# A two-layer transformer kernel on one core: the third batch's down products move out of the first attention unit into the order of the FFN chunks, with the first layer's front reordered

## The reference, cut to what matters

```
xn = layernorm(x)
attn: qkv = xn @ qkv_w + qkv_b   (16 heads of 64), causal softmax(q k / 8) v, @ out_w + out_b
ffn:  gate = xn @ w_gate / 127;  up = xn @ w_up / 127;  (silu(gate) * up) @ w_down / 127   (384 hidden)
x = x + attn + ffn
```

## Time and profile before

| | |
|---|---|
| median of 3 runs | 1658.24 us (1657.25 to 1658.27) |
| the profiled execution | 1658.69 us, span 1657.0 us |
| PE busy | 1636.4 us, 99% of the span |
| DVE, ACT, POOL busy | 80%, 61%, 54% |
| mean granted clock of PE | 0.999 |

### The profile page before, as it was taken

The page is one execution under the profiler, slowest core; times in us unless marked ns, Lnnn a source line. Parts: engine busy times, 40 slices in busy tenths (PEclk is TensorE's granted clock), DMA queues, the critical chain, the costliest instruction groups (busy, mean ns, idle before and its releaser), DMA issues.

```text
span 1657.0 us, 29205 instructions
## 1 busy us (share of the span) xinstructions
PE 1636.4 (99%) x9922; PEld 1043.9 (63%) x9922; DVE 1328.9 (80%) x2763; ACT 1006.7 (61%) x2025; POOL 888.1 (54%) x686
## 2 busy tenths in 40 slices
PE   8999999999999999999999999999999999999998
PEld 6756556655665566566656665665666767676767
DVE  6677777777777778777777777776999999999997
ACT  4456666656665666566656666666676657566562
POOL 3233333334333333433333433334999999999995
PEclk9999999999999999999999999999999999999999
DMA  8000000000000000000000000000000000000000
GB/s 182 26 1 1 2 1 1 1 2 1 1 1 1 1 2 1 1 1 1 1 1 1 1 2 1 1 27 1 1 1 7 7 1 8 5 4 7 1 8 13
DMA packets 30036, 13.55 MB, mean 8 GB/s; under 512 B 17066, under 2 KB 29380, under 8 KB 29892
## 3 DMA queue, kind: packets, MB, share of 16 engines
q1 hardware_dynamic: 29892, 11.70, 3.0%
HBM read 9.60 MB, written 2.10 MB: 7 GB/s over the span
## 4 chain that ended last, share of the span: by engine, by line
PE 92%; DVE 4%; ACT 1%; issue 1%; POOL 1%; DMA 0%; SPq 0%; DVEq 0%; ACTq 0%; POOLq 0%
PE pair L994 17%; PE flip L1011 16%; PE accum L1032 11%; PE pair L2739 8%; PE misc L959 7%; PE flip L2762 4%; PE misc L1078 4%; PE flip L2751 4%; PE misc L972 3%; PE accum L1056 3%; PE flip L2799 3%; PE accum L2751 2%; PE accum L2762 2%; PE accum L1060 2%; PE flip L2785 1%; PE flip L936 1%
## 5 line engine op out<-in xcount | busy, mean ns | idle before, releaser
L388 POOL TENSOR_SCALAR probs<-probs,recip 128x256 f32<-128x256 f32 (+5 forms) x448 | 331.3, 754 | 687.5 <-DVE recip L642 687.4
L463 ACT ACTIVATE probs<-pair,neg_max 128x768 f32<-128x768 f32 (+5 forms) x448 | 332.0, 749 | 208.4 <-DVE neg_max L624 208.4
L624 DVE TENSOR_REDUCE neg_max<-pair 128x1 f32<-128x768 f32 (+7 forms) x512 | 372.8, 754 | 31.4 <-PE pair L994 9.5
L1011 PEld LDWEIGHTS flip<-ident,probs 128*128 128x128 f32 x2048 | 228.0, 141 | 142.3 <-issue 64.7
L994 PE MATMUL pair<-qk_sb 64*128 64x512 f32 (+3 forms) x1536 | 291.6, 505 | 1.4 <-ACT probs L463 0.7
L1011 PE MATMUL flip<-ident,probs 128*128 128x128 f32 x2048 | 280.0, 277 | 1.8 <-ACT slots L425 1.8
L425 ACT ACTIVATE slots<-flip 128x512 f32<-128x512 f32 x320 | 183.6, 595 | 155.5 <-PE flip L1011 155.5
L615 DVE TENSOR_TENSOR pair<-pair,mask 128x128 f32<-128x128 f32 x512 | 137.2, 292 | 80.4 <-PE pair L994 80.3
L1032 PE MATMUL accum<-slots,v_sb 128*64 128x512 f32 (+3 forms) x1024 | 192.7, 519 | 0.0
L2739 PE MATMUL pair<-slow_sb,h_T 128*128 128x512 f32 x384 | 180.0, 594 | 1.2 <-ACT probs_last L463 1.0
L1571 POOL TENSOR_TENSOR prod<-xnT,qs 128x1024 f32<-128x1024 f32 (+3 forms) x32 | 180.2, 5638 | 0.9 <-DVE qs L2280 0.9
(11 more groups left out here) (230 smaller groups left out, 2539.7 us busy)
## 6 DMA issues: line engine op xcount, KB each, us to landing
out<-x SPq DMA_DIRECT2D x8, 256.0 KB, 2.3
x<-in_L_attn_x SPq DMA_DIRECT2D x3, 512.0 KB, 5.8
slow_sb<-in_L_attn_w_slow SPq DMA_DIRECT2D x3, 512.0 KB, 7.5
w_qk<-in_L_attn_qkv_w SPq DMA_DIRECT2D x2, 512.0 KB, 7.2
xn<-in_L_ffn_W SPq DMA_DIRECT2D x1, 1024.0 KB
x<-in_L_attn_x SPq DMA_DIRECT2D x2, 256.0 KB, 3.3
w_v<-in_L_attn_qkv_w SPq DMA_DIRECT2D x1, 512.0 KB, 7.5
bv_bc<-in_L_attn_qkv_b SPq DMA_DIRECT2D x1, 512.0 KB, 7.5
```

The costliest lines, as they stand in the source:

```text
L388: pool.tensor_scalar(part, part, recip[:, u % 2, row, h:h + 1], 0.0, ALU.mult, ALU.add).then_inc(scaled, 1)
L463: act.activation(dst, pair[h][:, lo:hi], ACT.Exp, bias=neg_max[:, u % 2, row, h:h + 1], accum_out=row_sum[:, u % 2, row, h:h + 1]).then_in ...
L624: dve.tensor_reduce(out=neg_max[:, u % 2, row, h:h + 1], in_=pair[h][:, lo:hi], axis=AX.X, op=ALU.max, negate=True).then_inc(max_ready, 1)
L1011: last = pe.transpose(flips[bank][:, P * k:P * (k + 1)], src[:, P * k:P * (k + 1)], ident[:])
```

## The change

It does seven things, all in the first layer:

1. PE: `branch(2)` leaves unit 0; its halves stand in the front, the first after the gate product of chunk (3, 1), the second after the last product. DVE's `add_branch(2)` leaves unit 0 likewise, in halves.
2. PE: `hidden` can issue the gate and the up product separately, and `flip_xn` a half at a time; projections, down products and transposes stand between the products.
3. PE: `project(0, 0, 1)` and `project(0, 1, 0)` come much earlier, with the wait for the q and k weights; the values products come earlier as well.
4. DVE: `norm` goes by halves, each with its own signal, so that transposes of a half wait for that half alone; `keep_lo` goes by halves; `statistics(2)` precedes `multiply(0, 0)`, and `statistics(3)` `multiply(1, 1)`.
5. ACT: `keep_hi` goes by halves; the order of silus and copies follows that of PE. A Silu of one column is put first.
6. POOL: `deviation(1)` and `deviation(2)` come before the wait for `out_b`, `deviation(3)` behind `add_bias(2)`; `add_bias(b)` waits for both halves of its own norm.
7. Waits of `flip_xn` are by half too: for batch 1 on the half's copy of batch 0, for later ones on the half's addition of two batches before.

No instruction is left out; one is added (the small Silu). The diff, without the bodies of `norm`, `keep_lo`, `keep_hi` and `hidden`, which get the half or the product as an argument and are otherwise as they were:

```diff
@@ POOL
             def add_bias(b):
-                pool.wait_ge(xn_ready, min(b + 2, B))
+                pool.wait_ge(xn_ready, 2 * b + 1)
...
+            deviation(1)
+            deviation(2)
             pool.wait_ge(small_loaded, 16)
-            for b in range(1, B):
-                deviation(b)
-                add_bias(b - 1)
-            add_bias(B - 1)
+            add_bias(0)
+            add_bias(1)
+            add_bias(2)
+            deviation(3)
+            add_bias(3)
@@ ACT
+            act.wait_ge(ident_made, 1)
+            act.activation(act_gate[:, 0:1], ident[:, 0:1], ACT.Silu)
             act.wait_ge(ints_loaded, 48)
...
             keep_hi(0)
             silu(0, 0)
             silu(0, 1)
-            keep_hi(1)
+            keep_hi(1, (0,))
+            keep_hi(1, (1,))
             silu(0, 2)
             keep_xnT(1)
             silu(1, 0)
             silu(1, 1)
-            keep_hi(2)
+            keep_hi(2, (0,))
+            keep_hi(2, (1,))
             silu(1, 2)
             keep_xnT(2)
+            silu(2, 0)
+            keep_hi(3, (0,))
+            silu(2, 1)
+            keep_hi(3, (1,))
+            silu(2, 2)
+            silu(3, 0)
+            keep_xnT(3)
             act.wait_ge(bq_scaled, 1)
-            silu(2, 0)
-            silu(2, 1)
-            keep_hi(3)
-            silu(2, 2)
-            keep_xnT(3)
-            silu(3, 0)
             keep_part(0, 1, 1)
@@ DVE
                 maximum(u, 7, 0)
-                if u == 0:
-                    add_branch(B - 2)
...
             statistics(1)
+            statistics(2)
             multiply(0, 0)
-            norm(1)
+            norm(1, 0)
+            norm(1, 1)
             multiply(0, 1)
-            keep_lo(1)
-            statistics(2)
+            keep_lo(1, 0)
+            keep_lo(1, 1)
+            dve.wait_ge(bq_scaled, 1)
+            keep_part(0, 0, 1)
             multiply(0, 2)
-            norm(2)
+            keep_part(0, 1, 0)
+            norm(2, 0)
+            norm(2, 1)
+            add_branch(0, (0,))
             multiply(1, 0)
-            add_branch(0, (0,))
+            statistics(3)
+            add_branch(0, (1,))
             multiply(1, 1)
-            add_branch(0, (1,))
-            keep_lo(2)
+            keep_lo(2, 0)
+            keep_lo(2, 1)
+            multiply(1, 2)
+            norm(3, 0)
+            norm(3, 1)
             dve.wait_ge(v_loaded, 32)
-            dve.wait_ge(bq_scaled, 1)
-            statistics(3)
-            multiply(1, 2)
-            norm(3)
+            keep_values(0, 0)
             multiply(2, 0)
-            keep_part(0, 0, 1)
             add_branch(1, (0,))
+            add_branch(1, (1,))
+            keep_lo(3, 0)
             multiply(2, 1)
-            add_branch(1, (1,))
-            keep_part(0, 1, 0)
-            keep_lo(3)
+            keep_lo(3, 1)
+            keep_values(0, 1)
             multiply(2, 2)
-            keep_values(0, 0)
             multiply(3, 0)
-            keep_values(0, 1)
+            add_branch(2, (0,))
             multiply(3, 1)
             multiply(3, 2)
+            add_branch(2, (1,))
@@ PE
+                    else:
+                        pe.wait_ge(xn_ready, 2 * b + f)
+                    if b == 1:
+                        pe.wait_ge((xnT_dve, xnT_act)[f], 1)
+                    elif b:
+                        pe.wait_ge(ffn_added, 2 * (b - 2) + f + 1)
...
                 score(u, 0, 0)
-                if u == 0:
-                    branch(B - 2)
...
-            flip_xn(0)
-            hidden(0, 0)
-            hidden(0, 1)
-            flip_xn(1)
-            hidden(0, 2)
-            hidden(1, 0)
+            flip_xn(0, (0,))
+            flip_xn(0, (1,))
+            hidden(0, 0, (0,))
+            hidden(0, 0, (1,))
+            hidden(0, 1, (0,))
+            hidden(0, 1, (1,))
+            flip_xn(1, (0,))
+            hidden(0, 2, (0,))
+            flip_xn(1, (1,))
+            pe.wait_ge(qk_loaded, 32)
+            project(0, 0, 1)
+            hidden(0, 2, (1,))
+            hidden(1, 0, (0,))
+            project(0, 1, 0)
             pe.wait_ge(xnT_act, 2)
             branch(0, (0,))
-            hidden(1, 1)
+            hidden(1, 0, (1,))
+            hidden(1, 1, (0,))
             branch(0, (1,))
-            flip_xn(2)
-            hidden(1, 2)
-            pe.wait_ge(qk_loaded, 32)
+            hidden(1, 1, (1,))
+            flip_xn(2, (0,))
+            flip_xn(2, (1,))
+            hidden(1, 2, (0,))
+            hidden(1, 2, (1,))
             pe.wait_ge(v_loaded, 32)
-            project(0, 0, 1)
-            hidden(2, 0)
+            project_values(0, 0)
+            hidden(2, 0, (0,))
+            hidden(2, 0, (1,))
             pe.wait_ge(xnT_act, 3)
             branch(1, (0,))
-            hidden(2, 1)
             branch(1, (1,))
-            project(0, 1, 0)
-            flip_xn(3)
-            hidden(2, 2)
-            project_values(0, 0)
+            flip_xn(3, (0,))
+            hidden(2, 1, (0,))
+            flip_xn(3, (1,))
+            hidden(2, 1, (1,))
+            hidden(2, 2, (0,))
+            project_values(0, 1)
+            hidden(2, 2, (1,))
+            hidden(3, 0, (0,))
+            project(0, 1, 1)
+            hidden(3, 0, (1,))
+            hidden(3, 1, (0,))
             pe.wait_ge(xnT_act, 4)
-            hidden(3, 0)
-            project_values(0, 1)
-            project(0, 1, 1)
-            hidden(3, 1)
+            branch(2, (0,))
+            hidden(3, 1, (1,))
             project(0, 0, 0)
-            hidden(3, 2)
+            hidden(3, 2, (0,))
+            hidden(3, 2, (1,))
+            branch(2, (1,))
```

More of the change, by code:

```diff
@@ L522, in keep_xnT, with keep_hi @@
                 act.activation(xnT[:, b, 512:1024], flips[1][:], ACT.Copy).then_inc(xnT_act, 1)
-            def keep_hi(b):
+            def keep_hi(b, halves=(0, 1)):
                 if b == 0:
@@ L531, in keep_hi @@
                     act.wait_ge(up_ready, NHID * (b - 1))
-                for f in range(2):
+                for f in halves:
                     act.wait_ge(xn_flipped, 2 * b + f + 1)
@@ L786, in first_norm, with norm @@
                 last.then_inc((xn_first, xn_ready)[f], 1)
-            def norm(b):
+            def norm(b, f):
                 dve.wait_ge(rstd_ready, b + 1)
@@ L791, in norm @@
                     dve.wait_ge(xn_flipped, 2 * (b - 1))
-                for r in range(ROWS):
+                for r in range(GB * f, GB * (f + 1)):
                     last = dve.tensor_scalar(xn[:, b % 2, r, :], x1[:, b, r, :], mv[:, b, r, 0:1], rstd[:, b, r:r + 1],
@@ L799, in keep_xnT, with keep_lo @@
                 dve.tensor_copy(xnT[:, b, 0:512], flips[0][:]).then_inc(xnT_dve, 1)
[L801 to L805, removed]
+            def keep_lo(b, f):
+                part = slice(512 * f, 512 * (f + 1))
+                dve.wait_ge(hi_kept, 2 * b + f)
+                dve.tensor_tensor(lo_T[b % 2][:, part], flips[f][:], hi_T[b % 2][:, part].bitcast(F32), ALU.subtract).then_inc(lo_dve, 1)
             def multiply(b, j):
@@ L879, in _, with flip_xn @@
             pe.transpose(pair[1][:, 512:512 + COLUMNS], stage[:], ident[0:COLUMNS, 0:COLUMNS]).then_inc(setup_flipped, 1)
[L881 to L886, removed]
+            def flip_xn(b, halves=(0, 1)):
+                for f in halves:
                     if b == 0:
                         pe.wait_ge((xn_first, xn_ready)[f], 1)
+                    else:
[4 more added lines that the diff above has]
+                        pe.wait_ge(ffn_added, 2 * (b - 2) + f + 1)
                     for r in range(GB):
@@ L891, in flip_xn, with hidden @@
                     last.then_inc(xn_flipped, 1)
-            def hidden(b, j):
+            def hidden(b, j, products=(0, 1)):
                 n = b * NHID + j
-                for h, w_T in enumerate((gate_T, up_T)):
+                for h in products:
+                    w_T = (gate_T, up_T)[h]
                     if h == 0 and n:
```

## The result

The changed kernel takes 1654.61 us (median of 12 runs, 1653.23 to 1656.12) where the one before takes 1657.79 (12 runs, 1657.21 to 1660.29) in the same sitting. The ratio is 0.9979, with a 95% interval from 0.9971 to 0.9987: faster by 0.2%, and by 3.2 us from median to median. The forecast was 1652.5, 2.1 us too low, with a range up to 1655.5.

The account below looks back on a forecast made before the run. TensorE (PE), busy 99% of the span, was taken as the bound. A gain of 7.2 less 1.55 for the clock, 5.65, gave 1653.0 from the profiled 1658.69 or 1652.6 from the median; forecast 1652.5, range 1650.3 to 1655.5.

Parts of the forecast that it names:

- Step (b): Front: branch(2) enters as 5.46 us of PE work, set against 8.29 idle; first scores at 62.1 instead of 66.78.
- the walk: New order stepped through with row timings, to unit 0's second score step: 67.7 against 75.12, gain 7.4 us.
- checkpoints: Front from 19.8: needed and ready times of PE steps, each operand there before its turn; stated margins 0.1 to 0.5.
- deviation(2) goes ahead of two bias additions: POOL in the front: deviation(2) precedes two additions of 2.4 each, which helps; no wait is added.
- Friction: Rival, front: a dozen handovers each 0.3 late lose 2.5 to 3.5 us of the gain; 1655.5, chance 0.18.
- a stop for xn over 1 us after 20: Sign in the front's PE timeline that the forecast is wrong: a gap over 1 us after 20.
- The first score after 64: Sign at the front's end that the forecast is wrong; first scores were expected near 62.
- Step (a): Unit 0: without branch(2) the second score step follows after 5.6 us instead of 8.34, gain 2.74; new PE gap 2.8.
- Slower: Rival: front doesn't take in branch(2), grows 5.46, unit 0 gives 2.74, second fall costs 1.55; 1662.5, chance 0.04.
- Step (c): Unit 0: one fall of the clock after the new 2.8 gap, 1.55 us; bounds nothing and twice that.
- No fall: Rival: the clock doesn't fall in unit 0, gain 7.2 to 7.4, time 1651.0; chance 0.2.
- The cross-check by balance: Front to second score step: 54.3 busy plus gaps 1.1, 0.1 and 2.7 from 10.97 gives 69.2, gain 5.9.

Follow-up runs that it names:

- e3: The changed kernel with branch(2) and its additions back in unit 0, other reordering kept: 1651.58 us, ratio 0.9962 to the kernel before.
- e4: The kernel before with only branch(2) and its additions moved to the front: 1661.11 us, ratio 1.0020 to the kernel before.
- e6: The changed kernel with branch(2) back in unit 0, add_bias(0) behind norm(1), and statistics(2) behind keep_lo(1): 1654.46 us, ratio 0.9976.
- e2: The changed kernel with 10 instead of 20 warm-up matmuls at the start: 1655.15 us, ratio 0.9980 to the kernel before.
- e1: The changed kernel with POOL's add_bias(0) waiting for both halves of norm(1): 1653.11 us, ratio 0.9968 to the kernel before.

## Why the prediction was right or wrong

**The direction and the place** were right: PE was the bound, the front held the idle time, and the stretch behind the second score step kept its length.

**Step (b), the walk**, gave 56.7 from the first product to the second step and it took 58.40. Its checkpoints behind 22 came in their order with no stop of PE between them, each 1.3 to 1.9 later from the first product than the walk had it, and the two new gaps were there (1.1 expected, 1.19 found; 2.8 and 2.64). The step that failed is "POOL: deviation(2) goes ahead of two bias additions ..., which helps ... No wait is added". A wait was taken away, that of add_bias(0) for norm(1), and I costed its removal at nothing. It cost norm(1) 2.14 and PE a stop of 1.57. The rival *Friction* named the cause ("DVE and POOL hindering each other in the new overlap"), but spread it over a dozen handovers of 0.3; it came as one stop. Of the signs named in advance, a stop for xn over 1 us after 20 is there. The first score after 64 is too (64.54), but only because the first product was 0.85 late.

The Trainium skill (Advanced Engine Details and Errata, "VectorE Performance Modes") states that the second SBUF port of VectorE is shared with GpSimd, so that GpSimd instructions and VectorE instructions that use both ports block each other. The trace agrees as far as it goes: the norm, from SBUF to SBUF, is stopped beside the addition, 2.48 for 0.35, while multiplies, which read PSUM, are not. No row shows which instructions use both ports, and POOL's 128x8 instruction of 1.72 stopped no norm, so that not every GpSimd instruction does it.

**Step (a)**, "branch(2) leaves unit 0 ... gain 2.74", is right as a size (5.68 instead of 8.34), but was added to (b) as if the front would take branch(2) in. The walk's own checkpoints have PE full from 19.8 on, so work put there has to be paid for. e3 shows the price: 4.0 in the front against 2.66 in unit 0. The forecast's total hid this, since it compared two whole orders and never asked what the move by itself gives. The rival *Slower* had the mechanism and put it on the wrong condition (that the front is not filled); filled or not, the move doesn't pay.

**Step (c), one fall of the clock in unit 0, 1.55**: none in the profiled execution and a clock below 1.0 in 3 of 12 runs. What the rival *No fall* says of the clock was the usual case for this kernel; its 1651.0 was not, since the collision ate the gain. A fall behind such a gap does occur (e4, 3.37 for 2.00 at 0.50); for how often it strikes I had no row. The kernel before was read from one execution too: its own fall at 25, whose 1.55 the walk wins back, is a matter of the run, since 32 of the 61 runs beside the experiments had a mean clock of 1.0. Between full-clock runs the gain is 64.15 − 1.55 − 58.40 = 4.20, and their median spans say the same, 1656.0 and 1651.8.

**The sum.** Against the walk's 7.4 for the profiled execution: 1.7 lost to (b), 0.85 because the first product started at 11.82 instead of 10.97, which makes the 4.9 by which the span is shorter. The time of the profiled execution is 2.8 longer than its span where it was 1.7 before, so 1658.69 − 1654.93 = 3.8 are left. That the time fell into the range was in part luck: in the profiled pair no clock was lost, and the 1.55 set aside for it stood in for the collision. The cross-check by balance, 5.9 against the 5.75 that came, looks better than the walk, by luck too: it missed a stop of 1.57 and had 54.3 of busy time where the profile after shows 49.97 + 3.04 = 53.01. One small misreading: of the nine stops that the prediction counts in the front, the 0.63 before the first scores is one, and five others are shown in the earlier trace rows, not four.

## What to carry to other kernels

A wait can be there for what it keeps apart, not for the data it orders: before relaxing one between POOL and DVE, look in the timeline at what will then run side by side. When a change moves work and reorders around it, price the move alone; work that covers another engine's latency is worth its place as long as the stretch it would go to has no idle time left. A gap that PE gains behind such a move costs its length, and in some executions a fall of the clock on top. And a base that is read from one profile may hold a loss that half of its runs don't have.

## What the runs showed of the hardware that was not expected

- POOL's addition of 128x1024 fp32 (2.35 to 2.40) stops a DVE tensor_scalar from SBUF to SBUF for its whole length, and isn't slowed itself. The eight norms of a batch took 2.13 to 2.15 in every kernel where no addition ran beside them, 4.16 to 4.29 with one beside them (in five kernels), and 5.77 with two (e6). POOL's 128x8 instruction (1.72) ran beside norms and didn't lengthen them.
- The 40 warm-up records at the start end between 7.7 and 9.2 in the twelve profiled executions that have them, and the first gate product starts at 10.85 to 11.82. Where they end at 8.6 or later, it starts 2.6 behind their end. That is nearly 1 us of scatter from the start alone, and it took 0.85 from this comparison's profiled pair. The granted clock reads 1.00 there in both; what differs is the rate, which rises from 6 or 7 matmul records in a microsecond to 11 at about 5 before and about 8 after. Half the warm-up is no cure (e2).
- An execution lasts 1.7 to 3.2 us longer than its span. The kernel before had 1.7 or 1.8 in 16 of the 21 runs beside e1 to e4, the changed one in 3 of 12, but the changed one with the short warm-up (e2) in all 11. What lies in it no profile here shows, and why the kernels differ is left open.
